# Conv phases of a two-layer mixture kernel: the decay factor of the scans in PSUM, sine and cosine parts on other engines, table operations in another place

## What is computed

```python
def sconv(x, phazor_c, last_conv_c):
    B, L, D = x.shape
    r = jnp.abs(phazor_c)
    p = jnp.tanh(r) * jnp.exp(1j * jnp.angle(phazor_c))
    prog = p[None, :] ** jnp.arange(L, dtype=jnp.float32)[:, None]
    filt_fft = jnp.fft.fft(prog, n=2 * L, axis=0)
    x_fft = jnp.fft.fft(x.astype(jnp.complex64), n=2 * L, axis=1)
    conv = jnp.fft.ifft(filt_fft[None] * x_fft, axis=1)[:, :L]
    conv = conv + last_conv_c[None, None, :] * prog[None] * p[None, None, :]
    return conv.real.astype(x.dtype)
...
h = jnp.einsum('blv,dv->bld', x, Win) + bin
def body(h, p):
    l1w, l1b, pr, pi, lr, li, scl, l2w, l2b, w1, b1_, w2, b2_ = p
    y = jax.nn.silu(layernorm(h, l1w, l1b))
    y = sconv(y, pr + 1j * pi, lr + 1j * li)
    h = h + y * scl
    y = layernorm(h, l2w, l2b)
    y = jax.nn.silu(jnp.einsum('bld,fd->blf', y, w1) + b1_)
    y = jnp.einsum('blf,df->bld', y, w2) + b2_
    return (h + y, None)
...
h = layernorm(h, lnl_w, lnl_b)
s = jnp.einsum('bld,vd->blv', h, Wout) + bout
...
x = x + s * _silu(_L1_ffn_ref(xn, ...))
```

## Time and profile before

| | us |
|---|---|
| median of 3 executions | 642.12 |
| lowest, highest | 641.61, 645.01 |
| the profiled execution | 643.55 |
| its span in the trace | 641.7 |
| busy in the span: TensorE | 598.7 |
| VectorE | 506.0 |
| ScalarE | 339.1 |
| GpSimd | 194.9 |

### The profile page before, as it was taken

How to read it: one execution, slowest core, us unless ns; L and a number is a source line. 1 busy time by engine, 2 the same in 40 slices (tenths; PEclk the granted TensorE clock), 3 DMA queues, 4 the chain that set the end, 5 groups by cost and what they waited for, 6 DMA issues and landing times. The chain is left out here.

```text
span 641.7 us, 8820 instructions
## 1 busy us (share of the span) xinstructions
PE 598.7 (93%) x2852; PEld 464.1 (72%) x2852; DVE 506.0 (79%) x932; ACT 339.1 (53%) x571; POOL 194.9 (30%) x303
## 2 busy tenths in 40 slices
PE   8969999999999999999999999999698899999775
PEld 6857887887888888888888888877566555555432
DVE  7998799897888788789788778677575787877655
ACT  6758477267438428627734752848362444445320
POOL 2422002001001000200200100489884666664334
PEclk9979999999999999999999999999796999999887
DMA  8802000210020030020010001460300000000015
GB/s 359 304 13 67 1 1 1 66 34 2 23 75 0 0 98 0 0 98 0 0 64 34 0 1 67 148 221 4 64 4 0 1 0 1 1 1 1 1 65 196
DMA packets 17194, 32.35 MB, mean 50 GB/s; under 512 B 3238, under 2 KB 3750, under 8 KB 17164
## 3 DMA queue, kind: packets, MB, share of 16 engines
q1 hardware_dynamic: 17164, 31.99, 14.3%
HBM read 24.63 MB, written 7.35 MB: 50 GB/s over the span
## 5 line engine op out<-in xcount | busy, mean ns | idle before, releaser
L857 DVE TENSOR_SCALAR_CACHE_REDUCE junk_d<-k_buf,cand 128x1376 int8<-128x1376 f32 x56 | 91.8, 1640 | 0.3
L650 ACT ACTIVATE junk_a<-k_buf,cand 128x1376 int8<-128x1376 f32 x56 | 80.5, 1437 | 0.6
L1197 PE MATMUL ps_a<-wd_hi,zt_hi 128*128 128x512 f32 (+1 forms) x176 | 71.9, 408 | 0.2 <-DVE zt_lo L976 0.2
L629 ACT ACTIVATE s_buf<-ps_a 128x1376 f32<-128x1376 f32 x16 | 21.1, 1318 | 93.9 <-PE ps_a L1164 89.4
L1197 PE MATMUL ps_a<-wd_hi,zt_lo 128*128 128x512 f32 (+1 forms) x176 | 69.2, 393 | 0.0
L1197 PE MATMUL ps_a<-wd_lo,zt_hi 128*128 128x512 f32 (+1 forms) x176 | 68.8, 391 | 0.0
L527 POOL TENSOR_TENSOR xres<-xres,gate 128x512 f32<-128x512 f32 x12 | 22.4, 1866 | 130.9 <-DVE gate L983 130.9
L519 POOL TENSOR_TENSOR rstd<-var_eps,expo 128x2 f32<-128x2 f32 x7 | 4.9, 706 | 164.9 <-DVE var_eps L779 164.9
L1164 PE MATMUL ps_b<-wu_hi,xt_hi 128*128 128x512 f32 (+1 forms) x192 | 52.4, 381 | 0.0
L1164 PE MATMUL ps_a<-wg_hi,xt_hi 128*128 128x512 f32 (+1 forms) x192 | 52.0, 379 | 0.0
L1164 PE MATMUL ps_a<-wg_lo,xt_hi 128*128 128x512 f32 (+1 forms) x192 | 50.7, 372 | 0.5 <-DVE wg_lo L762 0.4
(11 more groups left out here) (249 smaller groups left out, 1414.7 us busy)
## 6 DMA issues: line engine op xcount, KB each, us to landing
xres<-in_x SPq DMA_DIRECT2D x8, 512.0 KB, 3.3
out<-arena SPq DMA_DIRECT2D x16, 256.0 KB, 2.1
xin<-in_x SPq DMA_DIRECT2D x7, 512.0 KB, 4.0
x_scratch<-xres SPq DMA_DIRECT2D x6, 514.0 KB, 4.0
arena<-x_scratch SPq DMA_DIRECT2D x3, 1028.0 KB, 12.6
m_buf<-in_wg_t SPq DMA_DIRECT2D x2, 688.0 KB, 4.8
k_buf<-in_wg_t SPq DMA_DIRECT2D x2, 688.0 KB, 7.6
m_buf<-in_wu_t SPq DMA_DIRECT2D x2, 688.0 KB, 7.4
```

What stands on the lines that cost most here:

```text
L629: act.activation(s_buf[:, t, :], ps_a[:].rearrange("p a n -> p (a n)")[:, 0:INNER], ACT.Silu).then_inc(s_ready, 1)
L650: act.activation(junk_a[:], k_buf[:, 1, :], ACT.Sign, bias=c, scale=-1.0, accum_out=below[:, 1:2]).then_inc(act_step, 1)
L857: dve.tensor_scalar(junk_d[:], k_buf[:, 0, :], c, -float(DROP), ALU.is_lt, ALU.add, accum_out=e).then_inc(cnt_dve, 1)
L1197: last = pe.matmul(ps_a[:, t, :], zs, ws[0:rows, c, :], start=(c == 0 and n == 0), stop=(c == CHUNKS - 1 and n == 2))
```

## The change

- `decay` (new) copies the layer's `rho` column into the first column of the PSUM bank `bank2[c]`, behind `normed`, which has read the bank. The scans read their factor from there.
- The sine product of y runs on VectorE (`turn_imaginary`), the cosine product on GpSimd (`turn_real`), which waits until the sine product is done. The imaginary scan comes first.
- GpSimd's second product (`back_imaginary`) has its own function; `settled` is left out there.
- The three table operations of a phase stand together behind `back_imaginary`, and wait for `add_real` (in phase 0 for `into_h`).
- One of the 3 gate matmuls between centering and variances goes behind the variances.
- `rot_c` and `rot_s` become one tensor `rot`.

```diff
@@ -61,7 +61,7 @@
 PRODUCTS = 3 * KH
-GATES = (3, 6, 5, 8, 2, 2)
+GATES = (2, 7, 5, 8, 2, 2)
@@ -1375,8 +1375,7 @@
             lnr = sb("lnr", [P, HALVES, 8])
-            rot_c = sb("rot_c", [P, DEPTH, NB])
-            rot_s = sb("rot_s", [P, DEPTH, NB])
+            rot = sb("rot", [P, DEPTH, 2, NB])
             tbig = sb("tbig", [P, NB])
@@ -1419,6 +1418,7 @@
             ln_o = by_half("ln_o")
+            cv_d = by_half("cv_d")
             cv_wr = by_half("cv_wr")
@@ -1469,6 +1469,11 @@
+
+            def decays(c):
+
+
+                return bank2[c][:, 0:1]
@@ -1528,7 +1533,7 @@
                     co, si, t = (v.rearrange("p (a b) -> p a b", b=FINE)
-                                 for v in (rot_c[:, l, :], rot_s[:, l, :], tbig[:]))
+                                 for v in (rot[:, l, 0, :], rot[:, l, 1, :], tbig[:]))
                     steps = ((t, ci, fi, ALU.mult), (co, cr, fr, ALU.mult), (co, co, t, ALU.subtract),
@@ -1541,13 +1546,16 @@
-                def times_sin(l, c, src, ready, count, done):
-
-                    pool.wait_ge(ready[c], count)
-                    if src is y:
-                        pool.wait_ge(cv_wr[c], l + 1)
+                def turn_real(l, c):
+
+                    pool.wait_ge(cv_wi[c], l + 1)
                     settled(pool, pool_passed)
-                    pool.tensor_tensor(w_im[:, cs(c)], src[:, cs(c)], rot_s[:, l, :], ALU.mult).then_inc(done[c], 1)
+                    pool.tensor_tensor(w_re[:, cs(c)], y[:, cs(c)], rot[:, l, 0, :], ALU.mult).then_inc(cv_wr[c], 1)
+
+                def back_imaginary(l, c):
+
+                    pool.wait_ge(cv_ui[c], l + 1)
+                    pool.tensor_tensor(w_im[:, cs(c)], u_im[:, cs(c)], rot[:, l, 1, :], ALU.mult).then_inc(cv_b[c], 1)
@@ -1568,26 +1576,22 @@
                 root(0, 0)
-                pool.wait_ge(ln_w[0], 1)
-                tables_some(6, 8)
-                times_sin(0, 0, y, ln_o, 1, cv_wi)
-                times_sin(0, 0, u_im, cv_ui, 1, cv_b)
+                turn_real(0, 0)
+                back_imaginary(0, 0)
+                pool.wait_ge(h_ready[0], 2)
+                tables_some(6, 9)
                 for phase in range(1, PHASES):
...
                     feeds = phase < PHASES - 1
-                    if l < DEPTH:
-                        pool.wait_ge(h_ready[c], 2 * l + 1)
-                        tables_some(5 + 3 * phase, 6 + 3 * phase)
                     root(2 * l, c)
...
                     if l < DEPTH:
-                        tables_some(6 + 3 * phase, 7 + 3 * phase)
-                        pool.wait_ge(tb, N_SMALL + 6 * l + 6)
-                        times_sin(l, c, y, ln_o, 2 * l + 1, cv_wi)
-                        tables_some(7 + 3 * phase, 8 + 3 * phase)
-                        times_sin(l, c, u_im, cv_ui, l + 1, cv_b)
+                        turn_real(l, c)
+                        back_imaginary(l, c)
+                        pool.wait_ge(cv_ab[c], l + 1)
+                        tables_some(6 + 3 * phase, 9 + 3 * phase)
                     elif feeds:
@@ -1716,13 +1720,19 @@
-                def turn(l, c):
+                def decay(l, c):
+
+                    dve.wait_ge(ln_y[c], 2 * l + 1)
+                    dve.tensor_copy(decays(c), rho[:, l:l + 1]).then_inc(cv_d[c], 1)
+
+                def turn_imaginary(l, c):
                     dve.wait_ge(tb, N_SMALL + 6 * l + 6)
                     dve.wait_ge(ln_o[c], 2 * l + 1)
-                    dve.tensor_tensor(w_re[:, cs(c)], y[:, cs(c)], rot_c[:, l, :], ALU.mult).then_inc(cv_wr[c], 1)
+                    dve.tensor_tensor(w_im[:, cs(c)], y[:, cs(c)], rot[:, l, 1, :], ALU.mult).then_inc(cv_wi[c], 1)
...
                     w, u, ready, done = (w_im, u_im, cv_wi, cv_ui) if imaginary else (w_re, u_re, cv_wr, cv_ur)
+                    dve.wait_ge(cv_d[c], l + 1)
                     dve.wait_ge(ready[c], l + 1)
@@ -1730,13 +1740,13 @@
                         first = carry[:, j:j + 1]
-                    dve.tensor_tensor_scan(u[:, cs(c)], rho[:, l:l + 1].to_broadcast([P, NB]), w[:, cs(c)],
+                    dve.tensor_tensor_scan(u[:, cs(c)], decays(c).to_broadcast([P, NB]), w[:, cs(c)],
                                            first, ALU.mult, ALU.add).then_inc(done[c], 1)
...
                     dve.scalar_tensor_tensor(out=w_re[:, cs(c)], in0=u_re[:, cs(c)], scalar=pcol(l, C_SCL),
-                                             in1=rot_c[:, l, :], op0=ALU.mult, op1=ALU.mult).then_inc(cv_a[c], 1)
+                                             in1=rot[:, l, 0, :], op0=ALU.mult, op1=ALU.mult).then_inc(cv_a[c], 1)
@@ -1833,8 +1843,9 @@
                 normed(0, 0)
+                dve.wait_ge(rho_s, 1)
+                decay(0, 0)
                 take_means(w2[:], KH, 2 * DEPTH, w2_s)
-                dve.wait_ge(rho_s, 1)
                 for phase in range(PHASES):
@@ -1857,15 +1868,17 @@
                         normed(q, c)
+                        if l < DEPTH:
+                            decay(l, c)
                         if feeds:
...
                     if l < DEPTH:
-                        turn(l, c)
+                        turn_imaginary(l, c)
                     if feeds:
...
                     if l < DEPTH:
+                        scan(l, c, True)
                         scan(l, c, False)
-                        scan(l, c, True)
                         turn_back(l, c)
```

## The result

The changed kernel took 632.21 us (median of 4 executions, 631.43 to 633.7), the kernel before 642.77 us beside it (4 executions, 641.61 to 645.01): a ratio of 0.984, 95% interval 0.981 to 0.987. The changed kernel is faster; forecast were 631.3 us and a range of 628.0 to 636.5. The profiled execution took 631.43 us, its span 629.6, which is 12.1 less than the span before. Busy now: TensorE 593.6 (598.7 before), VectorE 487.0 (506.0), ScalarE 339.8, GpSimd 188.7.

What follows compares the result with a forecast made beforehand. A ring led by VectorE's scans, taking turns with GpSimd's products, was taken as the bound. Gains of 4.5 (phase 0), 5.6 (phases 1 to 5), 0.3 (phase 6) and 0.4 (behind phase 7), together 10.8, gave 631.3 us; range 628 to 636.5.

Steps and rivals of the forecast that it cites:

- VectorE's part: Scans with the PSUM operand run free of GpSimd, 1.25 us each; VectorE alone would give 2.4 us a phase.
- Decay copy at nothing: The 128x1 copy behind the normed rows, 0.1 to 0.3 us, costs nothing, covered by VectorE's wait for ScalarE's y.
- TensorE chain of 15.1: TensorE with the feed-forward chain is late next, so a phase cannot be shorter than 15.1 us.
- The terms of 2.19 and 6.09: Parts of a phase: product to feed-forward matmuls 2.19 us, variances to the next product 6.09 us.
- 5.49 later, with no idle time in front of it: Start of the feed-forward matmuls to the next phase's centering, read from phase 6: 5.49 us.
- VectorE's slack of 1.7: h is ready at 5.98 and the centering starts at 7.68, leaving VectorE 1.7 us of slack a phase.
- Tables with 0.65 to spare: Three table operations behind the add end at 9.65, the root is wanted at 10.3: hidden with 0.65 us to spare.
- Phase 0, 4.5: In phase 0 h comes earlier and TensorE's clock stays at 2.4 GHz; the next product comes 4.5 us earlier.
- The rival with the falling clock: TensorE's clock falls in phase 1 all the same; phase 0 gains 1.9 us, total 633.9 us; chance 0.20.
- Behind phase 7, 0.4: In the stage behind phase 7 h comes earlier but the feed-forward chain binds: 0 to 0.6 us gained, 0.4 taken.
- The median: The gain of 10.8 us from the profiled 643.55, carried to the median of 642.12, gives 631.3 us.
- The rival "GpSimd becomes the bound": Table operations behind the add take 2.24 us each and make the roots late: 647 us, slower; chance 0.05.

Runs made afterwards that it cites:

- Experiments 1: The changed kernel, but the scans read the decay factor from SBUF again, the copy into PSUM staying: 643.58 us against 642.61 for the kernel before, ratio 1.002.
- experiment 2: The kernel before with only the decay factor copied into PSUM and read there by the scans: 636.39 us against 642.61, ratio 0.989.
- experiment 4: The changed kernel with the old gate matmul placement, three between centering and variances: 632.74 us against 642.61 for the kernel before, ratio 0.985.
- experiment 5: The changed kernel with one or three idle VectorE steps between the add and the sum into h: 634.19 and 641.25 us, beside 641.18 for the kernel before.
- experiment 3: The changed kernel with the three table operations in their old places: 633.52 us against 642.61 for the kernel before, ratio 0.984.
- the second of before: The kernel before, unchanged, run alone for a second profile: 641.69 us, one execution.
- the transposes: The kernel before with 14 more TensorE transposes behind the gate matmuls of phase 0: 641.12 us against 641.18; once more, 640.77 against 641.7.

## Why the prediction was right, point by point

- **VectorE's part** held: the scans were put at 1.25 each and measured 1.26 to 1.28; the add's end at 5.20 behind the product, measured 5.18; the sum into h at 5.98, measured 5.96. VectorE's product on L1748 took 0.75, where about 0.9 was named as a sign, and GpSimd's second product ended at 3.83 and not 3.93. Experiments 1 and 2 show that the PSUM operand is what frees the scans.
- **Decay copy at nothing**: it takes 0.16 us. VectorE idles 0.43 for ScalarE's y behind it, so the cover named is there.
- **TensorE chain of 15.1**: it is the next to bind, but measured 14.82. The terms of 2.19 and 6.09 held (2.20, 6.09), and centering to variances went from 1.65 to 1.32 where 1.33 stood. The gate matmul gave only 0.24 of that (experiment 4); the rest is the start behind a wait, which the operand took away (1.66 to 1.56 in experiment 2). The term that was mis-sized is "5.49 later, with no idle time in front of it" for the centering: it is 5.21. In phase 6 of before the sum into h ends at 585.42, and the centering starts 0.06 behind it, at 585.48, 0.51 behind the start of the last gate matmul:

```profile
584.67 0.75 DVE L1762 SCALAR_TENSOR_TENSOR h<-arena,h 128x512 f32<-128x512 f32 x1
```

```profile
584.97 0.39 PE L1954 MATMUL ps_b<-row_r,ones_r 128*128 128x512 f32 x1
```

  With h in time it starts 0.24 behind that matmul. So it had waited some 0.27 for h. The view prints no idle time there, since the matmul ahead counts as running until 585.36 and the 0.12 left over are not printed. Phase 6 of before, from which the term was read, was still VectorE's. Times 5 this makes 1.4; phases 1 to 5 gave 6.85 where 5.6 stood, and phase 6 0.61 where 0.3 stood.
- **VectorE's slack of 1.7**: it is 1.4 (experiment 5). The 1.7 had been worked out from the centering at 7.68 and h at 5.98; those are 7.41 and 5.96, and the centering starts 0.05 behind h when it waits for it.
- **Tables with 0.65 to spare**: they have 0.37. They end 9.59 behind the product, where 9.65 stood, though the first starts earlier (5.38, inside the sum into h) and takes 1.51 and not 1.07; the root was wanted at 9.96 and not 10.3, as the chain was shorter.
- **Phase 0, 4.5**: measured 4.52, but of parts of other sizes. The add ends 5.05 behind the product and not 4.87, since the real scan waited 0.18 for GpSimd's product; TensorE waited 0.86 and not 0.7; the variances came at 486.86, 8.63 behind the product, near the 8.7 of the prediction (486.1 from 477.42). The clock stayed up, as forecast; the other three executions have the same mean clock, 0.974, as the traced one. That was nearly missed: with one VectorE step more (experiment 5) the clock fell, and so it did with the tables in their old places (experiment 3), both with a wait of 1.41. The rival with the falling clock had a chance of 0.20 and put the gain of phase 0 at 1.9; the kernel of experiment 5 with one step gained 1.7 there (19.35 to 17.66). What decides between up and down is not shown, so that the clock stayed up was in part luck.
- **Behind phase 7, 0.4**: from the product to the variances of phase 8 0.58 (8.99 to 8.41, from 602.21 and 590.46), and 0.35 more in the rest, which took 39.49 and 39.14. In the two traces in which the clock is down there for 6.8 us in place of 10.2, the second of before and that of experiment 4, the rest takes 37.74 and 37.72. So the change gave 0.58 there, and the rest goes mostly by the clock; for the 0.35 between the two traces with 10.2 us no cause is shown.
- **The median**: the sum was taken against one execution with a mean clock of 0.966, and carried to the median by subtracting 1.4. Against the executions of before with the higher mean clock the gain of the change is nearer 8.7 (640.9 to 632.2), against the others 11.7; these are estimates, as the times of before come from other sessions. The sum of 10.8 lies between, and the median of before with it. That the measured median is 0.9 from the forecast rests in part on two errors that go opposite ways: the chain taken too long, and the clock counted as if it fell in each execution. To that extent the nearness is luck.
- **The rival "GpSimd becomes the bound"** did not come true: the three tables last 4.21 from first start to last end (542.97 to 547.18), not 7.1.

## What to carry to other kernels

When an engine is freed, price the next ring by its own stretches, and look for waiting hidden between matmuls. Here they start 0.24 apart while each is shown for 0.39, so that a wait of 0.27 leaves a gap of 0.12 and the view prints nothing: the distance between starts tells it, the idle column doesn't. One operand in PSUM, if only a broadcast column, is enough to let a VectorE instruction run beside GpSimd. Ask of each gain that hangs on the clock in how many executions the clock falls before; one profile doesn't say it, and the mean granted clock of every execution says it only in part, since other stretches move the mean too.

## What was not expected of the hardware

- TensorE's clock in phase 1 hangs on more than the wait for h in front of the centering. It fell in the kernel before behind 2.93 and 2.89 us, behind 1.41 us in experiments 3 and 5 and behind 1.39 us in the first trace with the transposes. It stayed at 1.00 behind 1.40 us (the transposes once more), 0.87 us (experiment 4) and 0.86 us (the change). The same program with the transposes did both. Behind the longest waits it was not down the longest: behind 2.90 us, with three steps, it was below 1.00 only between 490 and 496.
- Phases 1 to 5 of the kernel before repeat to 0.04 us, within an execution and in four traces with and without the transposes (16.19 to 16.23). The start of the first layer moves by 2.5 us (24.4 and 21.9), and the stage behind phase 7 by 1.75 us in the same kernel (48.48 and 46.73), as the clock is down there for 10.2 or for 6.8 us. Differences of tenths are to be read from phases, not from the whole time.
- GpSimd's root of 128x8 took 1.63 us alone and 2.0 with a VectorE split beside it; the split, with two SBUF inputs, took its usual 0.68 in the middle of it. The product of 128x512 on GpSimd holds such a VectorE operation up until it ends (1.65 and 1.59 in place of 0.7); the root doesn't.
